# Gathers issued inside the routing stage, a LoRA product moved into the expert loop, and two pooling loads issued before the stage border

## The chip, the cores and the metric

The kernel runs on one core of a Trainium2 chip. A core has five engines that run side by side: PE (TensorE, matrix products), DVE (VectorE), ACT (ScalarE), POOL (GpSimd) and SP (SyncE, which here only issues DMAs). They talk through semaphores: an instruction may wait until a semaphore has reached a number, and raise one when it is done; a DMA raises one when its data has landed. The metric is device microseconds for one execution, lower is better. Times of before: 870.08 us, the median of 3 runs (869.97 to 871.64).

## The reference

Two layers work on x of 8 x 512 tokens with 512 channels. Layer 0 makes a LoRA feature of each token (by language), routes it to 2 of 8 experts with a capacity of 512 tokens each, and adds the experts' weighted outputs to x. Layer 1 is an attention-like pooling, followed by a quantised feed-forward network. Cut to the part that the change touches:

```
def _L0_ffn_ref(x, expert_embeddings, first_linear, second_linear):
    weights = _router(x, expert_embeddings)              # top 2 of 8, softmax
    ones = (weights > 0).astype(weights.dtype)
    cap_ones = jnp.where(jnp.cumsum(ones, axis=0) <= expert_capacity, ones, 0.0)
    caw = weights * cap_ones
    vals, idx = jax.lax.top_k(caw.T, expert_capacity)
    index = idx.reshape(-1)
    tokens = x_flat[index].reshape(E, expert_capacity, hidden)
    inter = jax.nn.relu(jnp.einsum('ech,eih->eci', tokens, first_linear))
    out = jnp.einsum('eci,ehi->ech', inter, second_linear) * vals[:, :, None]
    return jnp.zeros((n_tokens, hidden)).at[index].add(out.reshape(-1, hidden)).reshape(x.shape)
x = x + _L0_ffn_ref(_L0_cond_ref(x, ...), ...)           # _L0_cond_ref: LoRA, rank 16, plus embedding
x = _L1_cond_ref(x, ...)                                 # tanh scores, masked softmax, pooled / count
x = _L1_ffn_ref(x, ...)                                  # rmsnorm, int8 x ternary, gelu, int8 x ternary
```

## The kernel before

The program has four stages, each in a block of its own. At the end of a block every engine runs a DRAIN and then waits for all the others, so the next stage starts when the last engine has arrived.

**Routing.** The token features (64 LoRA coordinates and the language, 104 numbers a token) are computed from x for eight batches. The slots are then given in two halves, q = 0 and 1. For each half DVE chooses the experts (`choose`, which needs an exponential from ACT, `exps`), PE counts (`count`), DVE gives slots (`give_slots`), DVE and ACT build one-hot tables (`hot_lanes` on ACT), and PE inverts the map from token to slot (`find`). From that DVE makes `row_of_slot`, the token of each slot of each expert. POOL writes the features of a half to DRAM (L270) when they are complete, and waits at the end for both writes (L276, semaphore `feat_out`).

PE also computes, for each expert e, the product g of the first layer's weights with the LoRA matrix, 100 x 1024: `expand(e, n)` in two halves n of 512 columns, four fp32 products each (line L148). ACT stores its high part (`high_g`) and DVE its low part (`low_g`), so that later products run in a faster format with both parts. In the routing stage this is done for the experts 0 and 1.

**Experts.** At its start POOL gathers the feature rows of the experts 0 and 1 from DRAM with 4 indirect DMAs for each (L645). PE computes the product of expert 2 before it transposes the first gathered rows (`turn(0)`, L824). Then comes a loop over 8 experts and 8 blocks k of 128 inner channels: `inner_block` (L831, L832) makes 128 x 512 of the first layer, ACT and DVE split it into a high part (L728) and a low part (L793), and `out_block` (L844 to L846) adds 12 products of the second layer. From e = 1 on the loop also holds the product of expert e + 2, spread over the blocks by the table `G_AT`: `expand(e + 2, k)`, with one or two fp32 products behind the 12. The results are added to `x1_dram` by POOL's indirect DMAs (L659, semaphore `y_out`), and POOL waits for the last of them before the border.

**Pooling.** SP loads the masks (L949) and then two batches of x1 into `x_sum` (L954). DVE runs a chain of small operations (L1127 to L1154) that ends with the semaphore `setup`; PE waits for `setup` and for the first `x_sum` before its first transpose (L1035).

**Feed-forward.** 32 tiles of 128 tokens, not touched.

What sets the order is the written order on each engine: all engines run their instructions in the order of the text, and a waiting instruction holds back everything behind it on its engine.

Of the kernel before, what the change touches and what calls it, by code (L numbers as in the profile page):

```python
# [102 lines left out]
def build(nc, x, x_t, lang, kind, lora_a, lora_a_t, lora_b_t, embed_t, router_t, w_in_t, w_out_t,  # L103
# [7 lines left out]
    with ExitStack() as whole:  # L111
# [19 lines left out]

        l0 = whole.enter_context(ExitStack())
        row_of_slot = sb(l0, "row_of_slot", [P, EXPERTS * SB], U32)
        lora_b_sb = sb(l0, "lora_b_sb", [P, KD, STACK_1])
# [7 lines left out]
        feat_out, x1_init = sem("feat_out"), sem("x1_init")  # L142
        w_in_v = w_in_t.rearrange("e (p k) i -> e p k i", k=KD)
        w_out_v = w_out_t.rearrange("e (a k p) h -> e a p k h", a=2, p=P)

        def g_product(pe, e, n, k, bank):

            return pe.matmul(ps[0:STACK_1, bank, :], lora_b_sb[:, k, :],  # L148
                             w_in_sb[:, e % AHEAD, k, n * 512:(n + 1) * 512], start=k == 0, stop=k == KD - 1)


        with ExitStack() as a:
# [7 lines left out]
            xt = sb(a, "xt", [P, X_RING, KD, SEQ])  # L160
# [63 lines left out]
            with nc.Block() as block:  # L224
                @block.sync
                def _(sp):
# [5 lines left out]
                    def load_x(b):  # L232
                        if b >= X_RING:
                            sp.wait_ge(feats_mm, b - X_RING + 1)
                        sp.dma_start(xt[:, b % X_RING, :, :], xt_v[b]).then_inc(xt_in[b % X_RING], DMA)
# [24 lines left out]
                def _(pool):  # L260
# [15 lines left out]
                    pool.wait_ge(feat_out, DMA * PARTS)  # L276

                @block.scalar
                def _(act):
# [54 lines left out]
                    hot_lanes(0)  # L334
                    high_g(0, 0)
                    exps(1)
# [6 lines left out]
                def _(pe):  # L343
# [17 lines left out]
                    def feats(b):  # L361
# [4 lines left out]
                        for k in range(KD):  # L366
                            m = pe.matmul(ps[0:W, FEAT_T_BANK[b % 2], :], proj[:, b, k, :], xt[:, b % X_RING, k, :],
# [50 lines left out]
                    expand(0, 0)  # L418
                    expand(0, 1)
                    count(1)  # L420
                    expand(1, 0)
                    expand(1, 1)
                    find(1)

                @block.vector
                def _(ve):
# [123 lines left out]
                    ve.scalar_tensor_tensor(row_of_slot[:], spare[:], -1.0, token[:], ALU.add, ALU.add)  # L550
# [13 lines left out]
        with ExitStack() as a:  # L564
# [3 lines left out]
            rows = sb(a, "rows", [P, 2, SB, ROW])  # L568
# [15 lines left out]
            rows_in = [sem(f"rows_in{i}") for i in (0, 1)]  # L584
# [21 lines left out]
            with nc.Block() as block:  # L606
                @block.sync
                def _(sp):
# [9 lines left out]
                    for e in range(EXPERTS):  # L618
# [12 lines left out]
                        if e + AHEAD + 1 < EXPERTS:  # L631
                            n = e + AHEAD + 1
                            sp.wait_ge(g_mm, 2 * (n - AHEAD + 1))
                            sp.dma_start(w_in_sb[:, n % AHEAD, :, :], w_in_v[n]).then_inc(w_in_in[n % AHEAD], DMA)

                @block.gpsimd
                def _(pool):
                    pool.wait_ge(feat_out, DMA * PARTS)

                    def gather(e):  # L640
                        if e >= 2:
                            pool.wait_ge(rows_tr, e - 1)
                            pool.wait_ge(w_slot_ready, e - 1)
# [8 lines left out]
                    for e in range(EXPERTS):  # L652
                        if e + 2 < EXPERTS:
                            gather(e + 2)
# [803 lines left out]
```

## Time and profile before

| | |
|---|---|
| median of 3 runs | 870.08 us (869.97 to 871.64) |
| the profiled execution | 869.48 us |
| its span, first to last instruction | 867.3 us |
| granted TensorE clock, mean | 0.945 |
| PE busy | 760.5 us (88%) |
| DVE busy | 525.2 us (61%) |
| ACT busy | 503.6 us (58%) |
| POOL busy | 298.6 us (34%) |

The span is 2.2 us shorter than the execution that it was taken from; what lies around the span is not in the trace. All positions below are microseconds from the start of the span. The routing stage takes the first 86 us, the experts the time to 368.8 us, pooling the time to 601 us and the feed-forward network the rest. POOL's "DMA_INDIRECT" is the time in which POOL prepares a gather or scatter; the landing comes later. Names that end in q (POOLq) are the engine's sequencer. In the trace a product of line L148 appears as two MATMUL records.

### The profile page before, as it was taken

Reading aid. Unit: us, or ns where it says so; the run is one execution under the profiler, and the core shown is the slowest. Engines: PE = TensorE matmul, PEld = TensorE weight load, DVE = VectorE, ACT = ScalarE, POOL = GpSimd, SP = SyncE. Lnnn points to the kernel's source line nnn. Section 1 sums busy time; section 2 is a strip of 40 time slices with the busy share of each in tenths; the row PEclk is TensorE's granted clock in tenths of the full one; section 3 lists DMA queues with packets and bytes.
Section 4 is the critical chain, followed back from the end, with each engine's and each line's share of the span. In section 5 each row is a group of like instructions: output and inputs, shape, how many; then the busy total and the mean of one; then the engine's idle time right before and its main releaser. Section 6 shows DMA issues by size and latency. Waiting matters only on the chain. (4 is left out here: it accounts for less than half of the span.)

```text
span 867.3 us, 10854 instructions
## 1 busy us (share of the span) xinstructions
PE 760.5 (88%) x3794; PEld 492.9 (57%) x3824; DVE 525.2 (61%) x986; ACT 503.6 (58%) x714; POOL 298.6 (34%) x264
## 2 busy tenths in 40 slices
PE   6864899998999999246999999975799999999997
PEld 3331487776777777234777877763355555554553
DVE  2446344554544554132566565633899999999995
ACT  1144346753577788124655665522787777777783
POOL 0010324324224212213344444400354445544553
PEclk9987799999999999667999999987999999999999
DMA  7999359887558555331111120001012122122222
GB/s 231 373 400 336 123 202 335 268 288 205 170 134 211 153 146 132 48 128 50 49 49 48 50 98 1 1 1 36 6 57 73 61 74 74 62 65 70 74 64 82
DMA packets 42645, 109.03 MB, mean 126 GB/s; under 512 B 4320, under 2 KB 5104, under 8 KB 39392
## 3 DMA queue, kind: packets, MB, share of 16 engines
q1 hardware_dynamic: 35760, 94.84, 31.0%
q0 software_dynamic: 6320, 13.06, 8.1%
q8 instruction: 30, 0.49, 0.2%
q10 hardware_dynamic: 512, 0.45, 0.2%
q14 instruction: 23, 0.19, 0.1%
HBM read 88.59 MB, written 28.13 MB: 135 GB/s over the span
## 5 line engine op out<-in xcount | busy, mean ns | idle before, releaser
L1317 PE MATMUL ps<-ff_q,qt 128*128 128x512 bf16 x496 | 121.9, 386 | 8.4 <-DVE h L1382 6.3
L1343 PE MATMUL ps<-ff_q,ht 128*128 128x512 bf16 x498 | 114.5, 379 | 3.3 <-DVE ht L1399 2.6
L844 PE MATMUL ps<-w_h,inner_l 128*128 128x512 f32 x256 | 102.8, 402 | 3.6 <-DVE inner_l L793 3.6
L846 PE MATMUL ps<-w_h,inner_h 128*128 128x512 f32 x256 | 101.2, 395 | 0.0
L845 PE MATMUL ps<-w_l,inner_h 128*128 128x512 f32 x256 | 101.1, 395 | 0.0
L1303 POOL TENSOR_SCALAR hb<-h 128x2048 bf16<-128x2048 int8 x32 | 60.8, 1900 | 111.0 <-ACT h L1361 111.0
L659 POOL DMA_INDIRECT x_after_experts<-y,row_of_slot x32 | 51.5, 1609 | 134.6 <-DVE y L779 127.3
L1361 ACT ACTIVATE h<-h,to_q 128x2048 int8<-128x2048 f32 x32 | 64.1, 2002 | 44.1 <-DVE to_q L1413 44.1
L1382 DVE SCALAR_TENSOR_TENSOR h<-ps,scale,bias 128x1024 f32<-128x1024 f32 x64 | 81.6, 1279 | 9.1 <-PE ps L1317 9.0
L793 DVE SCALAR_TENSOR_TENSOR inner_l<-ps,inner_h 128x512 fp32r<-128x512 f32 x64 | 44.2, 691 | 70.1 <-ACT inner_h L728 69.6
L1317 PEld LDWEIGHTS ps<-ff_q,qt 128*128 128x128 bf16 x512 | 49.5, 99 | 63.9 <-DVE h L1382 7.6
L1343 PEld LDWEIGHTS ps<-ff_q,ht 128*128 128x128 bf16 x512 | 49.8, 98 | 62.7 <-DVE res L1422 1.6
L728 ACT ACTIVATE inner_h<-ps 128x512 fp32r<-128x512 f32 x64 | 38.0, 594 | 81.5 <-PE ps L832 81.1
L1387 DVE TENSOR_REDUCE mx<-h 128x1 f32<-128x1024 f32 x64 | 77.4, 1210 | 1.1 <-ACT h L1351 1.1
L1351 ACT ACTIVATE h<-h 128x1024 f32<-128x1024 f32 x64 | 67.1, 1049 | 16.1 <-DVE h L1382 16.1
L148 PE MATMUL ps<-w_in_sb,lora_b_sb 128*100 128x512 f32 x128 | 63.3, 617 | 9.7 <-PEq L224 9.7
L790 DVE TENSOR_TENSOR w_l<-w_raw,w_h 128x512 fp32r<-128x512 f32 x64 | 44.2, 690 | 45.2 <-ACT w_h L724 45.0
L1002 PE MATMUL ps<-x_h,prob_l 128*128 128x512 f32 x128 | 62.4, 488 | 6.5 <-ACT q L1097 6.4
L976 POOL TENSOR_TENSOR x_l<-x_sum,x_h 128x1024 fp32r<-128x1024 f32 x16 | 38.1, 2384 | 69.2 <-ACT x_h L1107 51.7
L1369 ACT ACTIVATE junk<-h 128x2048 bf16<-128x2048 f32 x32 | 61.1, 1911 | 1.0
L844 PEld LDWEIGHTS ps<-w_h,inner_l 128*128 128x128 f32 x256 | 49.1, 192 | 15.2 <-DVE inner_l L793 4.9
L846 PEld LDWEIGHTS ps<-w_h,inner_h 128*128 128x128 f32 x256 | 48.9, 191 | 10.8
(216 smaller groups left out, 1467.7 us busy)
## 6 DMA issues: line engine op xcount, KB each, us to landing
w_in_sb<-in_w_in_t SPq DMA_DIRECT2D x8, 2048.0 KB, 12.1
w_raw<-in_w_out_t SPq DMA_DIRECT2D x16, 1024.0 KB, 5.5
raw<-in_ff_t SPq DMA_DIRECT2D x16, 1024.0 KB, 7.5
xt<-in_x_t SPq DMA_DIRECT2D x8, 1024.0 KB, 9.4
x_after_experts<-in_x SPq DMA_DIRECT2D x8, 1024.0 KB, 18.0
x_sum<-x_after_experts SPq DMA_DIRECT2D x8, 1024.0 KB, 4.7
x<-x_after_experts SPq DMA_DIRECT2D x32, 256.0 KB, 2.7
out<-res SPq DMA_DIRECT2D x32, 256.0 KB, 2.0
```

Of the source, the lines that this page charges most:

```text
L148: return pe.matmul(ps[0:STACK_1, bank, :], lora_b_sb[:, k, :], w_in_sb[:, e % AHEAD, k, n * 512:(n + 1) * 512], start=k == 0, stop=k == KD ...
L844: pe.matmul(ps[:, s, :], inner_l[:, k % 2, c], w_h[:, k % RING, :], start=k == 0, stop=False)
L845: pe.matmul(ps[:, s, :], inner_h[:, k % 2, c], w_l[:, k % RING, :], start=False, stop=False)
L846: m = pe.matmul(ps[:, s, :], inner_h[:, k % 2, c], w_h[:, k % RING, :], start=False, stop=k == KI - 1)
L1002: pe.matmul(ps[:, NUM + j, :], prob_l[at_l], x_h[:, b % 2, l, :], start=first, stop=False)
L1317: m = pe.matmul(ps[:, f, :], qt[:, t, k, :], ff1_q[:, k, f * 512:(f + 1) * 512], start=k == 0, stop=k == KD - 1)
L1343: m = pe.matmul(ps[:, OUT[t3 % 2], :], ht[:, k, :], ff2_q[:, k, :], start=k == 0, stop=k == KF - 1)
L1351: act.activation(part, part, ACT.Gelu).then_inc(gelu, 1)
L1361: act.activation(h8[:, t1 % 2, :], h[:, t1 % 2, :], ACT.Copy, scale=to_q[:, t1 % 2:t1 % 2 + 1]).then_inc(h8_ready, 1)
L1369: act.activation(junk[:], h[:, t0 % 2, :], ACT.Square, accum_out=sq[:, t0 % 2:t0 % 2 + 1]).then_inc(h_sq, 1)
L1382: ve.scalar_tensor_tensor(h[:, t % 2, half], ff_bank[i], scale1[:, t:t + 1], bias1[:, half], ALU.mult, ALU.add).then_inc(biased, 1)
L1387: ve.tensor_reduce(mx[:, t % 2, i:i + 1], h[:, t % 2, i * HALF:(i + 1) * HALF], AX.X, ALU.max, apply_absolute_value=True).then_inc(h_max, 1)
```

## The change

The instructions that move, and what moves in memory with them:

- POOL issues the 8 gathers of the experts 0 and 1 at the end of the routing block, after `feat_out` and after a new semaphore `rows_known`, which DVE raises with `row_of_slot`. They no longer stand at the start of the expert block.
- ACT runs the second exponential `exps(1)` ahead of `high_g(0, 0)`; PE runs `count(1)` ahead of `expand(0, 1)`.
- PE runs `find(1)` ahead of `expand(1, 1)`.
- The product of expert 2 goes from the front of the expert block into the loop at e = 0, with its high and low parts.
- SP issues the first two `x_sum` loads at the end of the expert block, after a wait for all of `y_out`; the masks are loaded behind them, at the start of the pooling block.
- In memory, `rows` and `x_sum` live longer; two of the three buffers of x in the routing stage are now the `x_sum` buffers.

```diff
+        def gather(pool, e):
+            for s in range(SB):
+                pool.indirect_dma_start(
+                    rows[:, e % 2, s, :], None, feat_dram,
+                    bass.IndirectOffsetOnAxis(row_of_slot[:, e * SB + s:e * SB + s + 1], 0)).then_inc(rows_in[e % 2], DMA)
...
-            xt = sb(a, "xt", [P, X_RING, KD, SEQ])
+            xt = x_sum + [sb(a, "xt", [P, KD, SEQ])]
...
                     pool.wait_ge(feat_out, DMA * PARTS)
+                    pool.wait_ge(rows_known, 1)
+                    gather(pool, 0)
+                    gather(pool, 1)
...
                     hot_lanes(0)
+                    exps(1)
                     high_g(0, 0)
-                    exps(1)
                     high_g(0, 1)
...
                     expand(0, 0)
+                    count(1)
                     expand(0, 1)
-                    count(1)
                     expand(1, 0)
+                    find(1)
                     expand(1, 1)
-                    find(1)
...
-                    ve.scalar_tensor_tensor(row_of_slot[:], spare[:], -1.0, token[:], ALU.add, ALU.add)
+                    ve.scalar_tensor_tensor(row_of_slot[:], spare[:], -1.0, token[:], ALU.add, ALU.add).then_inc(rows_known, 1)
...
+                    sp.wait_ge(y_out, DMA * SB * EXPERTS)
+                    for b in (0, 1):
+                        load_x_sum(sp, b)
...
-                    pool.wait_ge(feat_out, DMA * PARTS)
-                    gather(0)
-                    gather(1)
                     pool.wait_ge(x1_init, DMA * BATCH)
...
-                    for n in (0, 1):
-                        high_g(AHEAD - 1, n, n)
                     take_rows(0)
...
-                            if k == 0 and 2 <= e <= EXPERTS - AHEAD + 1:
+                            if k == 0 and 1 <= e <= EXPERTS - AHEAD + 1:
                                 high_g(e + 1, 1)
-                            if k == 4 and 1 <= e <= EXPERTS - AHEAD:
+                            if k == 4 and e <= EXPERTS - AHEAD:
                                 high_g(e + 2, 0)
...
-                    low_g(AHEAD - 1, 0, 0)
                     take_rows(0)
-                    low_g(AHEAD - 1, 1, 1)
...
-                    pe.wait_ge(w_in_in[AHEAD - 1], DMA)
-                    for n in (0, 1):
-                        for k in range(KD):
-                            m = g_product(pe, AHEAD - 1, n, k, n)
-                        m.then_inc(g_mm, 1)
                     turn(0)
...
-                            if 1 <= e <= EXPERTS - AHEAD:
+                            if e <= EXPERTS - AHEAD:
                                 expand(e + 2, k)
...
                     sp.dma_start(mask[:], masks).then_inc(mask_in, DMA)
-                    for b in range(BATCH):
-                        if b >= 2:
-                            sp.wait_ge(x_trd, KD * (b - 1))
-                            sp.wait_ge(x_l_cp, 2 * (b - 1))
-                        sp.dma_start(x_sum[b % 2][:], x1_v[:, b * TPB:(b + 1) * TPB, :]).then_inc(x_in[b % 2], DMA)
+                    for b in range(2, BATCH):
+                        sp.wait_ge(x_trd, KD * (b - 1))
+                        sp.wait_ge(x_l_cp, 2 * (b - 1))
+                        load_x_sum(sp, b)
```

The order on PE from the last transposes of the routing stage to the first block of expert 0, before (L378 transposes features, L396 is `find`, L148 the LoRA product, L384 and L386 `count`, L224 and L817 the border, L824 `turn(0)`):

```order
L378 MATMUL ps<-const,feat_t 128x72 x8
L396 MATMUL ps<-ff_q 128x64 x32
L148 MATMUL ps<-w_in_sb,lora_b_sb 100x512 x8
L384 MATMUL ps<-chosen,ones_b 128x136
L386 MATMUL ps<-chosen,up_to_b 128x128
L148 MATMUL ps<-w_in_sb,lora_b_sb 100x512 x8
L396 MATMUL ps<-ff_q 128x64 x32
L224 UNCONDITIONAL_BRANCH
L817 UNCONDITIONAL_BRANCH
L148 MATMUL ps<-w_in_sb,lora_b_sb 100x512 x8
L824 MATMUL ps<-const,rows 100x128 x4
L831 MATMUL ps<-rows,g 128x512
```

The same place after the change, where L148 has become L158, L384 L405, L396 L417, L824 L831 and L831 L838:

```order
L399 MATMUL ps<-const,feat_t 128x72 x8
L417 MATMUL ps<-ff_q 128x64 x32
L158 MATMUL ps<-w_in_sb,lora_b_sb 100x512 x4
L405 MATMUL ps<-chosen,ones_b 128x136
L407 MATMUL ps<-chosen,up_to_b 128x128
L158 MATMUL ps<-w_in_sb,lora_b_sb 100x512 x8
L417 MATMUL ps<-ff_q 128x64 x32
L158 MATMUL ps<-w_in_sb,lora_b_sb 100x512 x4
L242 UNCONDITIONAL_BRANCH
L824 UNCONDITIONAL_BRANCH
L831 MATMUL ps<-const,rows 100x128 x4
L838 MATMUL ps<-rows,g 128x512
```

The second count now stands behind 4 products instead of 8, the second find ahead of the last 4, and the 8 products behind the border are gone. Two of them stand in the loop, on PE in expert 0 between the last products of `out_block(0, 0)` and `inner_block(0, 2)`:

```order
L849 MATMUL ps<-w_h,inner_l 128x512
L850 MATMUL ps<-w_l,inner_h 128x512
L851 MATMUL ps<-w_h,inner_h 128x512
L158 MATMUL ps<-w_in_sb,lora_b_sb 100x512 x2
L838 MATMUL ps<-rows,g 128x512
L839 MATMUL ps<-rows,g 128x512
```

The other six follow in the blocks k = 2 to 7 of expert 0, the way it was and is from expert 1 on. POOL before, from its last plain DMA of the routing stage, with what each waits for:

```order
L270 DMA token_features<-feat 128x1664 [waits placed,feat_cp]
L224 UNCONDITIONAL_BRANCH [waits feat_out,zero_out]
L636 UNCONDITIONAL_BRANCH [waits barrier_Pool_Activation_PE_DVE_SP_gather]
L645 DMA rows<-token_features,row_of_slot 128x104 [waits feat_out]
L645 DMA rows<-token_features,row_of_slot 128x104 x7
```

POOL after the change (L288 is the feature write, L164 a gather, L242 and L658 the border):

```order
L288 DMA token_features<-feat 128x1664 [waits placed,feat_cp]
L164 DMA rows<-token_features,row_of_slot 128x104 [waits rows_known,feat_out,zero_out]
L164 DMA rows<-token_features,row_of_slot 128x104 x7
L242 UNCONDITIONAL_BRANCH
L658 UNCONDITIONAL_BRANCH [waits barrier_Pool_Activation_PE_DVE_SP_gather]
L164 DMA rows<-token_features,row_of_slot 128x104 [waits w_slot_ready,rows_tr,x1_init]
```

All eight gathers now stand ahead of the border.

## Rows read from the trace of the kernel before

**Rows 1.** Windows of the trace; the columns are named in the row that is shown first.

```profile
core 0: us, PE busy (x) PEld busy (x) DVE busy (x) ACT busy (x) POOL busy (x), PEclk, DMA share, GB/s
77.00:86.10 9.10, 0.00 (x0) 0.00 (x0) 5.77 (x10) 0.39 (x1) 0.00 (x0) 0.50 1.01 360
86.10:89.30 3.20, 3.15 (x4) 1.27 (x5) 0.09 (x2) 0.00 (x0) 2.03 (x2) 0.50 0.90 283
100.60:106.30 5.70, 5.69 (x13) 4.46 (x14) 1.76 (x3) 0.04 (x1) 0.00 (x0) 0.50 0.00 0
123.00:156.00 33.00, 33.00 (x136) 24.52 (x135) 15.92 (x27) 20.33 (x38) 10.46 (x8) 1.00 0.86 293
```

**Rows 2.** Timeline of PE: start us, us, engine, line, what, [idle before, releaser].

```profile
56.28 8.21 PE L148 MATMUL ps<-w_in_sb,lora_b_sb 128*100 128x512 f32 x16
64.39 0.23 PE L384 MATMUL ps<-chosen,ones_b 128*128 128x136 bf16 x1
...
86.15 8.63 PE L148 MATMUL ps<-w_in_sb,lora_b_sb 128*100 128x512 f32 x16 [9.65 <-PEq L224]
94.66 0.65 PE L824 MATMUL ps<-const,rows 128*100 128x128 f32 x4
```

**Rows 3.** Timeline of ACT, end of the routing stage.

```profile
53.47 1.91 ACT L315 ACTIVATE ff_q<-ff_q 128x2048 bf16<-128x2048 bf16 x1
61.10 0.59 ACT L324 ACTIVATE g<-ps 64x512 fp32r<-64x512 f32 x1 [5.72 <-PE ps L148]
...
62.07 0.21 ACT L319 ACTIVATE gap_exp<-gap 128x16 f32<-128x16 f32 x1
...
68.74 4.78 ACT L312 ACTIVATE ff_q<-lane_id_b,minus_lo 128x128 bf16<-128x128 bf16 x16 [3.14 <-DVE minus_lo L521]
```

**Rows 4.** Timeline of DVE, end of the routing stage.

```profile
62.38 0.18 DVE L491 TENSOR_SCALAR kept<-gap_exp 128x16 f32<-128x16 f32 x1 [9.88 <-ACT gap_exp L319]
...
74.08 0.19 DVE L537 COPY feat<-slot 128x32 f32<-128x32 f32 x1
...
77.09 0.19 DVE L550 SCALAR_TENSOR_TENSOR row_of_slot<-spare,token 128x32 uint32<-128x32 f32 x1
```

**Rows 5.** Timeline of POOL, both sides of the border between the stages.

```profile
74.82 0.54 POOL L270 DMA_DIRECT2D token_features<-feat  x1 [22.99 <-DVE feat L537]
86.85 1.05 POOL L645 DMA_INDIRECT rows<-token_features,row_of_slot  x1 [11.49 <-POOLq L224]
...
95.75 0.95 POOL L645 DMA_INDIRECT rows<-token_features,row_of_slot  x1 [0.30 <-issue]
```

**Rows 6.** Line L270, both feature writes: issue to landing.

```profile
DMA to landing us min/median/max: 7.9/9.0/10.2
```

**Rows 7.** Line L224, the border after routing: names, count, ns, start us.

```profile
L224 POOLq DRAIN  x1: 645/645/645, 85.2 to 85.2; - x1
```

**Rows 8.** Line L606, the border after the experts.

```profile
L606 POOLq COMPARE_BRANCH  x1: 41/41/41, 363.1 to 363.1; - x1
L606 POOLq DRAIN  x1: 5273/5273/5273, 363.3 to 363.3; - x1
```

**Rows 9.** Timeline of PE, expert 0: the first second-layer product.

```profile
100.61 0.79 PE L844 MATMUL ps<-w_h,inner_l 128*128 128x512 f32 x1 [1.66 <-DVE inner_l L793]
```

**Rows 10.** Timeline of PE, expert 1: one part of a LoRA product in the loop.

```profile
137.05 1.02 PE L148 MATMUL ps<-w_in_sb,lora_b_sb 128*100 128x512 f32 x2
...
138.13 0.39 PE L832 MATMUL ps<-rows,g 100*128 100x512 f32 x1
138.37 0.60 PE L824 MATMUL ps<-const,rows 128*100 128x128 f32 x4
```

**Rows 11.** Timeline, start of the pooling stage.

```profile
369.15 49.92 SPq L954 DMA_DIRECT2D x_sum<-x_after_experts  x4
...
371.80 0.18 DVE L1154 CAST at_i<-at_f 128x32 int32<-128x32 f32 x1
...
375.04 1.94 PE L1035 MATMUL ps<-const,x_sum 128*128 128x128 f32 x8 [22.10 <-DMA x_sum<-x_after_experts]
```

More of the change, by code:

```diff
@@ L130, in build, with load_x_sum @@
         att_in = sem("att_in")
+        x_sum = [sb(whole, f"x_sum{i}", [P, TPB, D]) for i in (0, 1)]
+        x_in = [sem(f"x_in{p}") for p in (0, 1)]
+        x1_v = x1_dram[0:N_TOK, :].rearrange("(p t) d -> p t d", t=TILES)
+        def load_x_sum(sp, b):
+            sp.dma_start(x_sum[b % 2][:], x1_v[:, b * TPB:(b + 1) * TPB, :]).then_inc(x_in[b % 2], DMA)
         l0 = whole.enter_context(ExitStack())
         row_of_slot = sb(l0, "row_of_slot", [P, EXPERTS * SB], U32)
+        rows = sb(l0, "rows", [P, 2, SB, ROW])
         lora_b_sb = sb(l0, "lora_b_sb", [P, KD, STACK_1])
@@ L142, in build @@
         feat_out, x1_init = sem("feat_out"), sem("x1_init")
+        rows_known = sem("rows_known")
+        rows_in = [sem(f"rows_in{i}") for i in (0, 1)]
         w_in_v = w_in_t.rearrange("e (p k) i -> e p k i", k=KD)
@@ L634, in _ @@
                             sp.dma_start(w_in_sb[:, n % AHEAD, :, :], w_in_v[n]).then_inc(w_in_in[n % AHEAD], DMA)
+                    sp.wait_ge(y_out, DMA * SB * EXPERTS)
+                    for b in (0, 1):
+                        load_x_sum(sp, b)
                 @block.gpsimd
                 def _(pool):
-                    pool.wait_ge(feat_out, DMA * PARTS)
[L640 to L643, printed above, removed]
-                        for s in range(SB):
-                            pool.indirect_dma_start(
-                                rows[:, e % 2, s, :], None, feat_dram,
-                                bass.IndirectOffsetOnAxis(row_of_slot[:, e * SB + s:e * SB + s + 1], 0)).then_inc(rows_in[e % 2], DMA)
-                    gather(0)
-                    gather(1)
                     pool.wait_ge(x1_init, DMA * BATCH)
@@ L653, in _ @@
                         if e + 2 < EXPERTS:
-                            gather(e + 2)
+                            pool.wait_ge(rows_tr, e + 1)
+                            pool.wait_ge(w_slot_ready, e + 1)
+                            gather(pool, e + 2)
                         for s in range(SB):
@@ L796, in _ @@
                                 take_y(e - 1)
-                            if k == 0 and 2 <= e <= EXPERTS - AHEAD + 1:
+                            if k == 0 and 1 <= e <= EXPERTS - AHEAD + 1:
                                 low_g(e + 1, 1)
@@ L800, in _ @@
                                 weights(e)
-                            if k == 4 and 1 <= e <= EXPERTS - AHEAD:
+                            if k == 4 and e <= EXPERTS - AHEAD:
                                 low_g(e + 2, 0)
@@ L896, in build @@
         with ExitStack() as a:
-            x_sum = [sb(a, f"x_sum{i}", [P, TPB, D]) for i in (0, 1)]
             x_tr = sb(a, "x_tr", [P, 2, SEQ])
@@ L923, in build @@
             qb = sb(a, "qb", [P, TPB, KD, P], BF16)
-            x_in = [sem(f"x_in{p}") for p in (0, 1)]
             mask_in = sem("mask_in")
```

23 lines of the change are left out of this document (9 added, 14 removed).

## The prediction

> **What bounds the kernel now.** I read the windows first, then the timelines of the engines around the two stage borders that the change touches, then the borders' own rows. In the expert loop PE is the bound: from 123 to 156 us it is busy all 33.00 us at full clock [rows 1]. An operation added to PE in that loop costs its whole length, one taken away elsewhere gains only if PE waited for it. At the two borders PE is idle. From 77 to 86.1 us it does nothing while the DMA engines are fully busy (share 1.01) [rows 1]; it starts the product of expert 2 at 86.15 and the first transpose of gathered rows at 94.66 [rows 2]. At the other border it waits 22.10 us until 375.04, at last for the load of x_sum [rows 11]. So the change is three sums: when `turn(0)` can start, what the loop gets longer, and when the pooling stage can start.
>
> **The routing stage gets shorter by 3.4 us, as far as DVE.** DVE stood 9.88 us for the second exponential [rows 4], which ACT ran at 62.07, behind the high part that PE released at 61.10 [rows 3]. ACT is free at 53.47 + 1.91 = 55.4 and can now run it there. DVE then has `chosen` about 2 us later, near 57.7. That is no longer what ends last: `count(1)` now waits for PE, which is in `expand(0, 0)`. Its end releases ACT at 61.10, so the count now starts at about 61.0, against 64.39 [rows 2, 3]: 3.4 us sooner. DVE's chain from there is unchanged, so the last copy into the features moves from 74.08 to 70.7 and POOL's feature write from 74.82 to 71.4 [rows 4, 5]. ACT's second `hot_lanes` waits for the high part of (0, 1) (4 products of 0.86 us behind the count, then two copies of 0.59: 65.8) instead of for DVE until 68.74 [rows 3], so 2.9 us sooner; `find(1)` no longer has 4 products ahead of it that could hold it; so `row_of_slot` comes at 77.28 - 2.9 = 74.4 [rows 4]. The moved `expand(1, 1)` runs after it, from 73.7 at the latest to 80.6 (4 products of 1.7 us, if the clock has fallen), and its low part is done by 83.5; both lie beside POOL's work, below.
>
> **The border after routing: 2.3 us sooner for PE.** In before POOL passes its wait for the features at 85.0 and drains from 85.2 for 0.645 us [rows 7]; PE starts 86.15, 0.3 after the drain. So the landing of the second feature write holds this border: 74.82 + 10.2 = 85.0 [rows 5, 6]. The two writes took 7.9 and 10.2 us in the same full DMA traffic, median 9.0; issued at 71.4, the second lands at 79.3 to 81.6, and I take 80.4. `rows_known` (74.4) is then long there. POOL now issues 8 gathers before it can reach the border: 86.85 to 95.75 + 0.95 = 96.70, so 9.85 us [rows 5], plus 0.3 ahead of the first: 80.4 + 0.3 + 9.85 = 90.55. What stood behind the border, with only the first four gathers needed for `turn(0)`, now stands ahead of it with all eight. Then comes 0.15 and the drain. Its price with gathers before it is in no row. Two rows bound it: 0.645 us after the routing stage's 7 POOL DMAs (2 of features, 5 of zeros) [rows 7], and 5.27 us after the experts' 64 (32 gathers, 32 scatters), though the last had landed when it began [rows 8]. Per DMA that is 0.092 and 0.082 us, near enough to one law, so for 15 I take 1.3. With 0.3 to PE the border opens at 92.3, against `turn(0)` at 94.66 before: -2.3 us. The ends: landing 79.3 and a drain of 0.65 give 90.55, -4.1; landing 81.6 and a drain of 5.3 give 97.5, +2.8.
>
> The Trainium skill bears on the landing ("DMA: Bandwidth & Descriptors", section on queues, rings and completion order): each DMA engine takes turns between the rings that have work, a packet at a time. By that rule POOL's write isn't queued behind SP's backlog, and 3.4 us earlier in means about as much earlier out; if it were first in, first out over both queues, it would land with the backlog at 85. The 7.9 us of the first write, in the middle of that backlog, agree with the rule [rows 6].
>
> **From turn(0) to the first second-layer product: 0.5 us shorter.** Before, 94.66 to 100.61, 5.95 us [rows 2, 9]. Gone from it are ACT's high parts and DVE's low parts of expert 2, which stood between the steps; each such step is some 0.6 us on ACT [rows 3]. Against that the transposes and the first two products now run at the lower clock, since PE has idled since 77 and was at 0.50 there [rows 1]. Bounds 0 and 1.0 us; I take 0.5. The low clock of the first block (0.50 from 100.6 to 106.3 [rows 1]) stays about as long; each microsecond more or less of it is half a microsecond, so +-0.9.
>
> **The loop gets longer by 6.9 us.** Expert 0's blocks take over 8 fp32 products. In expert 1 one stands from 137.05 with two first-layer products behind it, the second at 138.13 and the next work at 138.37 [rows 10]: 1.32 less two of 0.24 = 0.84, and 0.86 if the two take the 0.23 that most take. 8 x 0.86 = 6.9 us. Before, they ran from 86.15 to 94.66 beside the gathers, where PE would have waited anyway: taking them from there gains nothing beyond the 2.3 above. In the loop nothing hides them: PE is the bound, and each stands behind the 12 products of an `out_block`, so none fits into the one wait of expert 0, 1.66 us [rows 9]. ACT and DVE have their parts of expert 2 in expert 0 and 1, as they have for later experts, in stretches where PE is busy without a gap [rows 1]. Bounds 6.7 and 7.7 (one product at the lower clock).
>
> **The border after the experts: 3.6 us sooner.** The wait for `y_out` ends at 363.1, but POOL's drain holds the border until 363.3 + 5.27 = 368.5 [rows 8]. SP issued x_sum at 369.15, after the masks, and PE started at 375.04 [rows 11], 5.9 later. SP now waits for `y_out` itself, issues at 363.2 and has x_sum at 369.0, under the drain. What is late next is `setup`: DVE ends it at 371.80 + 0.18 = 371.98 [rows 11], 3.2 us after the border. PE then starts at 372.05, -3.0. Eight DMAs fewer in this block take 8 x 0.08 = 0.65 off the drain, by the same law: -3.6. If the drain is fixed, -3.0. SP's two issues, 0.4 us each, end before 364.2, so SP is not late. The masks move behind x_sum; POOL needs them only behind ACT's first pass over x_sum, which itself waits for PE's first products.
>
> **Sum.** -2.3 - 0.5 + 6.9 - 3.6 = +0.5 us, against the profiled 869.48 us: 870.0. The median of the three runs is 0.6 above that execution, 870.08, so the forecast is 870.6 us.
>
> **Rivals.**
>
> *The drain is dear once there were gathers (slower).* For it: the only long drain stands behind indirect DMAs, none stands behind few of them. Against it: the count explains both rows. It decides from about 2.6 us of drain on (+1.3 us in the sum). At 5.3 us the routing border moves by +4.0 and the second keeps its 5.27 (+0.6): 875.2.
>
> *The feature write lands with the backlog, at 85.0 (slower).* `turn(0)` is then at 85.0 + 11.9 = 96.9, +4.6: 875.2. Against it is the first write's 7.9 us.
>
> *The routing is not shortened (slower).* If the count still ran at 64.4 (a lower clock of PE in `expand(0, 0)`, say), the feature write would stay at 74.8 and all of POOL's chain be 3.4 later: 874.0. Against it: rows 2 and 3 show ACT idle where the exponential goes.
>
> *The border is quicker than I have it (faster).* Landing at 79.3 (-1.1), a drain that doesn't grow (-0.65), the higher clock back sooner (-0.9): 868.0. For it: each part lies within its bound; against: they have to come together.
>
> **How the numbers follow.** The forecast's case has 0.60, the dear drain 0.17, the backlog 0.05, no shortening 0.06, the quick border 0.12. The first has a range of its own, 868.6 to 872.8. What this kernel's measurement can tell from no change is 0.2%, 1.7 us. Of the forecast's 0.60, 0.44 fall within that, 0.13 above it and 0.03 below. So faster 0.03 + 0.12 = 0.15, same 0.44, slower 0.13 + 0.28 = 0.41. The range runs from 868.0 to 875.2.
>
> **What will show it.** The count at 61.0, and DVE's wait of 9.88 us split in two of some 3 us, the second for PE; the feature write at 71.4, the first gather at 80.7 and the last at 89.6; POOL's drain at the first border 1.3 us, at the second 4.6; the first transpose of rows at 92.3; expert 0 longer by 6.9 us, the other experts as long as before; x_sum issued right behind the last scatter's landing, and PE's first transpose there released by DVE's setup, not by a DMA. I am wrong if the drain doesn't follow the count of DMAs, or if expert 0 grows by much less than 6.9.

## The result, and the profile after

| | kernel before | changed kernel |
|---|---|---|
| median, same chip, 7 runs each | 870.41 us (868.44 to 871.64) | 875.97 us (871.79 to 877.70) |
| ratio of after to before | | 1.006, 95% interval 1.004 to 1.008 |
| profiled execution: span | 867.3 us | 875.0 us |
| `turn(0)` starts | 94.66 | 98.24 |
| first second-layer product of expert 0 | 100.61 | 103.94 |
| last second-layer product of expert 7 | 352.55 | 364.11 |

The change costs 0.6%, about 5.5 us where 0.5 was forecast, and the time lies 0.8 us above the range. In the two profiled executions the difference is 7.7 us: 3.6 up to `turn(0)`, -0.25 from there to the first second-layer product, 8.2 in the loop, -3.9 from the start of its last product to the end. The medians differ by 5.6; the profiled execution of the changed kernel is one of its slower ones (877.18).

Timeline of DVE after (start us, us, engine, line, what, [idle before, releaser]), answering [rows 4]:

```profile
57.37 0.17 DVE L512 TENSOR_SCALAR kept<-gap_exp 128x16 f32<-128x16 f32 x1 [3.10 <-ACT gap_exp L340]
...
63.47 0.44 DVE L525 TENSOR_TENSOR_SCAN running<-not_first,ps 128x136 f32<-128x136 f32 x1 [4.14 <-PE ps L407]
...
72.82 0.19 DVE L558 COPY feat<-slot 128x32 f32<-128x32 f32 x1
...
76.10 0.19 DVE L571 SCALAR_TENSOR_TENSOR row_of_slot<-spare,token 128x32 uint32<-128x32 f32 x1
```

The wait of 9.88 us has split in two as forecast, the second one for PE. The count was expected at 61.0 and its result is used at 63.47. This execution runs 1.4 us late before the chain starts (the first feature write goes out at 49.4 against 48.05); the other microsecond is the chain's own.

Timeline of POOL after, answering [rows 5]:

```profile
73.56 0.54 POOL L288 DMA_DIRECT2D token_features<-feat  x1 [20.37 <-DVE feat L558]
85.98 1.05 POOL L164 DMA_INDIRECT rows<-token_features,row_of_slot  x1 [11.89 <-DMA token_features<-feat]
...
94.85 0.94 POOL L164 DMA_INDIRECT rows<-token_features,row_of_slot  x1 [0.30 <-issue]
```

Line L288, both feature writes from issue to landing ([rows 6] before), and line L242, the border after routing ([rows 7] before; name, count, ns, start):

```profile
DMA to landing us min/median/max: 8.2/9.9/11.6
```

```profile
L242 SPq DRAIN  x1: 122/122/122, 83.2 to 83.2; - x1
L242 POOLq DRAIN  x1: 9011/9011/9011, 89.0 to 89.0; - x1
```

The write goes out 1.3 us sooner than before and lands at 73.56 + 11.6 = 85.1, where it landed before (85.0). The first gather is at 85.98 and the last ends at 95.79. POOL's drain ends at 97.96, 2.2 us later. The row starts at 89.0 although POOL still issues gathers then, so its length is no measure of the wait; its end is.

Timeline of PE after, the first transpose of rows, the first second-layer product and one LoRA product in expert 0 ([rows 2, 9, 10] before):

```profile
98.24 1.07 PE L831 MATMUL ps<-const,rows 128*100 128x128 f32 x4 [17.77 <-PEq L242]
...
103.94 0.79 PE L849 MATMUL ps<-w_h,inner_l 128*128 128x512 f32 x1 [0.56 <-DVE inner_l L800]
...
114.08 1.02 PE L158 MATMUL ps<-w_in_sb,lora_b_sb 128*100 128x512 f32 x2
114.53 0.79 PE L838 MATMUL ps<-rows,g 128*128 128x512 f32 x1
```

Windows of the two traces from the first to the last of those products, first of before, then of after. The columns are us, busy us and instructions of each engine, granted clock of PE, DMA share, GB/s:

```profile
100.61:352.60 251.99, 247.11 (x1002) 186.44 (x1002) 123.17 (x204) 157.64 (x269) 69.98 (x53) 0.98 0.65 193
```

```profile
103.94:364.16 260.22, 255.35 (x1018) 189.70 (x1018) 126.05 (x208) 160.21 (x274) 70.16 (x53) 0.98 0.63 189
```

The loop has 16 PE instructions more, the 8 fp32 products. PE idles as long as before (4.88 and 4.87 us) and is busy 8.2 us longer. Not all of that is the products. Windows of before and of after, behind the same stall of 2.9 us in expert 3:

```profile
198.50:201.90 3.40, 3.35 (x9) 2.77 (x10) 1.88 (x3) 0.00 (x0) 3.05 (x2) 0.50 0.93 264
```

```profile
208.10:214.90 6.80, 6.13 (x15) 4.80 (x16) 2.47 (x5) 0.51 (x1) 3.89 (x3) 0.50 1.03 264
```

The granted clock falls to 0.50 (1.2 GHz) for 3.4 us in one execution and for 6.8 in the other.

The border after the experts ([rows 8, 11] before): line L625 first, then the timeline of the start of pooling.

```profile
L625 POOLq COMPARE_BRANCH  x1: 44/44/44, 374.5 to 374.5; - x1
L625 POOLq DRAIN  x1: 4622/4622/4622, 374.7 to 374.7; - x1
```

```profile
374.52 0.82 SPq L137 DMA_DIRECT2D x_sum<-x_after_experts  x2
379.55 0.33 SPq L946 DMA_DIRECT2D mask<-in_masks  x1
382.59 0.18 DVE L1150 CAST at_i<-at_f 128x32 int32<-128x32 f32 x1
...
382.82 1.54 PE L1031 MATMUL ps<-const,x_sum 128*128 128x128 f32 x6 [18.32 <-DVE at_i L1150]
```

This step came out as forecast: x_sum is issued under the drain, the drain is 0.65 us shorter with 8 DMAs fewer, PE is released by DVE's setup. From the wait's end to PE it is 8.3 us, against 11.9.

### The profile page after: what moved, and what is told of

Read it like the earlier page. It is cut to its first block and busy times, and to the rows that moved or that the text cites. A ratio compares the mean times of both kernels' runs of the same rounds, so it can differ in the third digit from the quotient of the medians.

```text
span 875.0 us, 10854 instructions
## 1 busy us (share of the span) xinstructions
PE 765.8 (88%) x3794; PEld 494.1 (56%) x3824; DVE 525.1 (60%) x986; ACT 503.4 (58%) x714; POOL 298.3 (34%) x264
## 5 line engine op out<-in xcount | busy, mean ns | idle before, releaser
L1378 DVE SCALAR_TENSOR_TENSOR h<-ps,scale,bias 128x1024 f32<-128x1024 f32 x64 | 81.6, 1279 | 9.0 <-PE ps L1313 8.9
L158 PE MATMUL ps<-w_in_sb,lora_b_sb 128*100 128x512 f32 x128 | 65.0, 623 | 0.0
L164 POOL DMA_INDIRECT rows<-token_features,row_of_slot x32 | 31.4, 980 | 73.7 <-DVE w_slot L773 54.2
## 6 DMA issues: line engine op xcount, KB each, us to landing
w_in_sb<-in_w_in_t SPq DMA_DIRECT2D x8, 2048.0 KB, 12.4
```

The lines of the kernel that those rows point to most:

```text
L1378: ve.scalar_tensor_tensor(h[:, t % 2, half], ff_bank[i], scale1[:, t:t + 1], bias1[:, half], ALU.mult, ALU.add).then_inc(biased, 1)
```

## The experiments

Each kernel ran in five rounds beside the kernel before, on one of three chips, where the kernel before had medians of 870.73 us (`only_loads`, `only_order`, `only_loop`, `copies_held`), 871.25 (`product_routing`, `gather_split`, `before_held`, `all_four`) and 871.67 (`two_edits`, `gathers_behind`). A ratio is to the kernel before, with its 95% interval. Microseconds "less than" or "above" another version are differences of medians; where the two ran on different chips the ratios are the safer comparison. "Profile" is one execution of each; times in it are us of its span.

**The three parts alone, on the kernel before.** First the pooling loads (`only_loads`):

```diff
+                    sp.wait_ge(y_out, DMA * SB * EXPERTS)
+                    for b in (0, 1):
+                        load_x_sum(sp, b)
```

The pooling block keeps its loads from the third batch on, and `x_sum` lives as long as in the changed kernel.

> The kernel before with one part of the change: SP waits for all of y_out and issues the first two x_sum loads before the border after the experts. Theory (POOL's drain still 5.27 us for 64 DMAs, then DVE's setup is what ends last): PE's first transpose 3.0 us sooner relative to the last scatter's landing, released by DVE; 3.0 us less in all, 867.4 against 870.4. Rival (the early loads are worth nothing, since PE waits for the setup at much the same time, or the drain gets longer with SP's loads beside it): within 0.5 us of before.

Measured: 868.0 us, ratio 0.9971 (0.9948 to 0.9994), so -2.5 us. In the profile POOL's wait ends at 362.5, its drain is 5273 ns as before, and PE starts 8.9 us behind the wait, 3.0 less than before:

```profile
371.39 1.97 PE L1041 MATMUL ps<-const,x_sum 128*128 128x128 f32 x8 [19.39 <-DVE at_i L1160]
```

The early loads are worth 3 us, and the other 0.65 of the 3.6 comes from the eight gathers that have left the block.

Then the routing stage's order (`only_order`):

```diff
                     hot_lanes(0)
-                    high_g(0, 0)
                     exps(1)
+                    high_g(0, 0)
...
                     expand(0, 0)
-                    expand(0, 1)
                     count(1)
+                    expand(0, 1)
                     expand(1, 0)
-                    expand(1, 1)
                     find(1)
+                    expand(1, 1)
```

> The kernel before with one part of the change: the second exponential before the first high part on ACT, the second count one half product earlier and the second find ahead of the last four products on PE. Theory A (POOL's second feature write lands when SP's eight copies of x are nearly through, whenever it is issued): issued near 71.5, landed at 84 to 85.5, the border after routing where it was, within 1 us of before. Theory B (landing follows the issue by 8 to 10 us, as I predicted): landed at 80 to 81.6, the border near 83.5 (then held by DVE's low parts), about 2.5 to 3 us less in all.

Measured: 871.12 us, ratio 1.0007 (0.9985 to 1.0029): nothing. In the profile the write goes out at 72.08, 2.7 us sooner than before, and takes 12.4 us. Line L270, both writes, then PE:

```profile
DMA to landing us min/median/max: 8.4/10.4/12.4
```

```profile
85.62 9.31 PE L148 MATMUL ps<-w_in_sb,lora_b_sb 128*100 128x512 f32 x16 [6.72 <-PEq L224]
96.04 0.65 PE L824 MATMUL ps<-const,rows 128*100 128x128 f32 x4 [1.11 <-DMA rows<-token_features,row_of_slot]
```

It lands at 84.5, 0.5 us sooner than before. Most of what DVE wins is lost in the flight. The rest is lost behind the border: PE starts 0.5 us sooner, but the fourth gather lands 9.7 us behind the start of the first (7.8 before), and `turn(0)` is at 96.04 against 94.66.

Then the product (`only_loop`), which leaves the place behind the border and goes into expert 0, with its high and low parts (not shown):

```diff
-                    for n in (0, 1):
-                        for k in range(KD):
-                            m = g_product(pe, AHEAD - 1, n, k, n)
-                        m.then_inc(g_mm, 1)
...
-                            if 1 <= e <= EXPERTS - AHEAD:
+                            if e <= EXPERTS - AHEAD:
                                 expand(e + 2, k)
```

> The kernel before with one part of the change: the product of expert 2 and its parts inside the loop at e = 0, the gathers still behind the border. Theory (eight fp32 products of 0.86 us on a full PE; turn(0) still released by the landing of the first four gathers at 94.6): 6.9 us more, less 0.5 us for the shorter chain behind turn(0), and up to 0.9 more if PE's clock comes back later: 876.0 to 878, that is +6 to +7.5. Rival (the larger clock loss of the changed kernel is what costs, and the products themselves mostly fit beside waits of PE): +1 to +3.

Measured: 881.3 us, ratio 1.0113 (1.0088 to 1.0137), so +9.8 us (7.7 to 11.9): more than I expected. In its profile `turn(0)` is at 94.71, as before, since the gathers hold it now:

```profile
94.71 1.09 PE L820 MATMUL ps<-const,rows 128*100 128x128 f32 x4 [18.75 <-DMA rows<-token_features,row_of_slot]
```

So the product behind the border was free, and in the loop it is not.

**What the product costs.** Twelve profiles give the loop's length and, within it, how long the granted clock stood at 0.50:

| kernel | loop us | at 0.50, us |
|---|---|---|
| all_four, before_held, product_routing | 249.2, 249.3, 249.2 | 3.1, 3.2, 3.2 |
| only_loads | 249.5 | 3.8 |
| before, only_order | 251.9, 251.9 | 9.1, 9.1 |
| gathers_behind, two_edits | 252.7, 252.9 | 11.3, 11.6 |
| product inside: copies_held | 256.8 | 4.0 |
| product inside: gather_split | 259.3 | 9.6 |
| product inside: changed kernel, only_loop | 260.2, 260.3 | 12.0, 12.2 |

Without the product the loop grows from 249.2 to 252.8 over 8.2 us of low clock, 0.44 us for each. At equal low clock (4.0, 9.6, 12.0) the kernels with the product inside are longer by 7.2, 7.1 and 7.1 us. The forecast had 6.9. The changed kernel's other 1.3 of 8.2 us is 2.9 us more of low clock, and the product is not what brings it: behind the stall `copies_held` has none and `gather_split` 3.4 with the product inside, `gathers_behind` and `two_edits` have the 6.8 without it. It differs from profile to profile. That still doesn't explain all 9.8 us of `only_loop`, whose interval begins 0.6 above the 7.1. Its profiled span is 11.1 us longer than that of the kernel before: 8.4 lie in the loop (7.1 and 1.3 as above), 0.4 from the loop's last product to PE's first transpose of pooling, and 2.5 behind that, where the two programs have the same text. From that transpose to the end the twelve profiles spread from 491.7 to 494.8 us, the kernel before at 492.3, `only_loop` at 494.8. So about 2.5 us of the surplus lie outside the code that was edited; why that stretch varies stays open.

**The copies held** (`copies_held`). On the changed kernel, SP lets the last four of its eight copies of x wait until the feature write has landed:

```diff
+                        if b == 4:
+                            sp.wait_ge(feat_out, DMA * PARTS)
                         sp.dma_start(x1_rows
```

> The changed kernel, but SP issues only four of its eight copies of x to x1 before it waits for feat_out; the other four come behind the feature write. Theory A (the feature write is slowed by the copies beside it): the second write lands 5 to 8 us after its issue, at 79 to 81, the gathers start there and turn(0) comes 4 to 6 us sooner than in the changed kernel; 870 to 872 in all. Theory B (what delays the landing is POOL's own queue, or the write itself): landing still 10 to 12 us after the issue, 876 as the changed kernel.

Measured: 872.12 us, ratio 1.0015 (0.9999 to 1.0031), 3.9 us less than the changed kernel. Timeline of POOL, then line L290 (both feature writes), lines L242 and L164 (the gathers, from the start of their issue to landing):

```profile
70.84 0.54 POOL L290 DMA_DIRECT2D token_features<-feat  x1 [19.39 <-DVE feat L560]
76.56 1.05 POOL L164 DMA_INDIRECT rows<-token_features,row_of_slot  x1 [5.19 <-DMA token_features<-feat]
...
85.45 0.95 POOL L164 DMA_INDIRECT rows<-token_features,row_of_slot  x1 [0.30 <-issue]
```

```profile
DMA to landing us min/median/max: 4.9/6.4/8.0
```

```profile
L242 POOLq DRAIN  x1: 12847/12847/12847, 79.5 to 79.5; - x1
```

```profile
DMA to landing us min/median/max: 6.2/6.5/7.1
```

The write now takes 4.9 us instead of 11.6: the copies beside it are what slows it. That it goes out sooner in this execution is not the reason: in `gather_split` it goes out at 70.92, beside the copies, and takes 11.7. This is theory A, and `turn(0)`, at 92.66, is 5.6 us sooner. But the border opens only at 92.4, 6 us behind the last gather's end (86.4). The gathers in turn fly beside the held copies, 6.2 to 7.1 us, the last landing at 91.7; the drain ends 0.7 us behind that. A drain that counts DMAs would have ended at about 87.7, by the forecast's 1.3. So with gathers before it POOL's drain lasts until they have landed. The last held copy lands at 91.7 too, but it isn't what the drain waits for: in the kernel before the drain is over at 85.9 and the eighth copy lands at 87.95.

**The gathers split** (`gather_split`). On the changed kernel the second four gathers go behind the border:

```diff
                     gather(pool, 0)
-                    gather(pool, 1)
...
+                    gather(pool, 1)
                     pool.wait_ge(x1_init, DMA * BATCH)
```

> The changed kernel with the four gathers of the second batch moved behind the border; the first four stay in the routing stage. Theory A (the barrier waits until the gathers issued before it have landed): the fourth gather ends at about 90.8, lands at about 92.5, the drain ends about 0.8 us later, and turn(0) is at about 93.5 instead of 98.2; the second four, issued from 94 on, are landed long before their turn at 138. Time about 871.3, 4.5 us under the changed kernel. Rival B (the drain costs by the number of DMAs issued in the block, 0.08 us each): it saves 0.3 us beside the 5 us of issuing, turn(0) at 93.0. Rival C (POOL is not what holds the barrier): turn(0) stays within 1 us of 98.2 and the time within 1 us of 876.

Measured: 870.03 us, ratio 0.9985 (0.9969 to 1.0002), 6 us less than the changed kernel.

```profile
L242 POOLq DRAIN  x1: 5659/5659/5659, 84.6 to 84.6; - x1
```

```profile
90.54 1.07 PE L831 MATMUL ps<-const,rows 128*100 128x128 f32 x4 [12.90 <-PEq L242]
```

The fourth gather ends at 88.3, the last landing in the trace before the border is at 89.75, the drain ends at 90.3. First gather to `turn(0)` is 7.1 us instead of 12.3: four gathers' issue of 1.25 us each, and 0.2. The rest of the 7.7 us by which `turn(0)` is sooner is the write, which lands at 82.6 in this execution. Rival C is out. A and B lie only 0.5 us apart here, so this run doesn't tell them apart; `copies_held` does.

**The product in the routing stage** (`product_routing`). On the changed kernel:

```diff
                     find(1)
                     expand(1, 1)
+                    expand(2, 0)
+                    expand(2, 1)
...
-                            if e <= EXPERTS - AHEAD:
+                            if 1 <= e <= EXPERTS - AHEAD:
                                 expand(e + 2, k)
```

> The changed kernel with the LoRA product of expert 2 taken out of the loop and put at the end of the routing stage, behind the halves of expert 1, where the profile after the change has TensorE idle from 80.5 to 98.2 us. Everything else stays. Theory A (the product inside the loop is what the loop pays for, and the routing stage can hide it): the product takes 8.5 us at the granted clock of that stretch, so TensorE is done at about 89.5 and VectorE at about 92, both before the gathers' drain ends at 98.05; turn(0) stays at 98.2; the loop is shorter by 7 to 8 us (first out product to last product start 260.2 to about 252.5), time about 868.5 (1.5 to 2.5 us under the kernel before, 7 to 8 under the changed one). Rival B (the barrier waits for the product's halves): turn(0) moves to 100 or later and the gain is 5 us or less, 871 or more. Rival C (the loop's surplus is TensorE's clock and not the product): the loop shortens by under 5 us.

Measured: 867.95 us, ratio 0.9964 (0.9950 to 0.9978), 8.0 us less than the changed kernel.

```profile
75.86 12.19 PE L158 MATMUL ps<-w_in_sb,lora_b_sb 128*100 128x512 f32 x24
97.68 1.06 PE L835 MATMUL ps<-const,rows 128*100 128x128 f32 x4 [9.64 <-PEq L242]
```

All the products run in what was PE's idle time and end at 88.1, 9.6 us before PE is wanted. The loop is 11.0 us shorter in the profile; at 0.44 us for each us of low clock, 3.9 of that is 8.9 us less at 0.50, and 7.1 the product.

**The copies held, on the kernel before** (`before_held`), with the same two new lines:

> The kernel before with one edit: the last four of SyncE's eight copies of x wait until the feature write has landed. Theory A (the write is slowed by those copies, and the border waits for the write): it lands at about 80 instead of 85.0 (issued 74.8, 4.9 us in the held variant of the changed kernel), the border then waits for VectorE until about 82.7, and turn(0), with the product of 8.5 us in front of it, comes at about 91.5 instead of 94.7: time 867 to 868, 3 us under the kernel before. Rival B (the copies held end later than the border and delay what follows, the gathers above all): turn(0) within 1 us of 94.7, time 870 to 871.

Measured: 877.76 us, ratio 1.0075 (1.0051 to 1.0099): 6.5 us slower where I expected 3 faster. Both theories missed; B's place was right, its price far too low. The border (line L224), the timeline of SP, and that of PE:

```profile
L224 POOLq DRAIN  x1: 645/645/645, 80.7 to 80.7; - x1
...
L224 SPq DRAIN  x1: 123/123/123, 87.7 to 87.7; - x1
```

```profile
59.20 23.96 SPq L255 DMA_DIRECT2D x_after_experts<-in_x  x5
83.20 2.04 SPq L256 DMA_DIRECT2D kind_i<-in_kind  x1
```

```profile
88.12 8.80 PE L148 MATMUL ps<-w_in_sb,lora_b_sb 128*100 128x512 f32 x16 [9.90 <-PEq L224]
102.89 1.09 PE L826 MATMUL ps<-const,rows 128*100 128x128 f32 x4 [5.97 <-DMA rows<-token_features,row_of_slot]
```

The write lands at 80.5, in 3.7 us, and POOL is at the border at 80.7. But SP, which issues its four copies and four small loads only then, comes at 87.7 and now holds it. The first gather starts at 88.8, 2.0 us later than before, and from there to `turn(0)` it takes 14.1 us instead of 7.8, as the gathers fly beside the held copies. The transfer is not gone, it has moved onto the gathers. In the changed kernel SP stays clear of the path, since the border waits for the gathers anyway.

**Three edits together** (`all_four`, the changed kernel with `product_routing`, `gather_split` and `copies_held`):

> The changed kernel with three edits together: expert 2's LoRA product at the end of the routing stage, the second four gathers behind the border, and the last four of SyncE's eight copies of x held until the feature write has landed. Theory A: the write lands at about 76, the four gathers are issued from 76.6 to 81.5 and landed by 87, TensorE's products end at about 87 and VectorE's part at about 90, so that turn(0) is at 90 to 91 (98.2 in the changed kernel, 94.7 before); the loop is 7 to 8 us shorter than the changed kernel's; the second border keeps its 3.6 us. Time 861 to 863. Rival B (what is won at the border comes back in the loop as waits for weights, since the copies and the gathers now lie beside the weight loads): 866 or more, with new waits of TensorE for weights in the loop.

Measured: 859.33 us (858.74 to 859.82), ratio 0.9863 (0.9842 to 0.9885): 12 us faster than the kernel before, 1.4%, and the fastest version. Line L242 and PE:

```profile
L242 POOLq DRAIN  x1: 9765/9765/9765, 78.5 to 78.5; - x1
L242 SPq DRAIN  x1: 122/122/122, 84.2 to 84.2; - x1
...
L242 DVEq DRAIN  x1: 1425/1425/1425, 87.4 to 87.4; - x1
```

```profile
89.14 0.62 PE L837 MATMUL ps<-const,rows 128*100 128x128 f32 x4 [2.86 <-PEq L242]
```

POOL is done at 88.3 and DVE, with the low parts of expert 2, at 88.8: the two sides meet, and PE waits 2.9 us instead of 17.8. No wait for weights has come into the loop.

**Without holding the copies** (`two_edits`, the `all_four` version without the two `copies_held` lines):

> The changed kernel with two of the three edits of the fastest version so far (859.3 us): expert 2's LoRA product at the end of the routing stage, and the second four gathers behind the border. SyncE's copies of x are not held. Theory A (the held copies win only what the feature write lands sooner, the rest of that version's gain is from the two other edits): the write lands at about 84.5, the four gathers run from 85.3 to 90, they have landed at about 92 and the barrier ends at about 92.5 (6.9 us behind the first gather in the run with the split gathers alone), so turn(0) at about 92.7 against 89.1 with the copies held; the loop is 249.2 us. Time 862.5 to 864, 3 to 4 us over the fastest. Rival B (holding the copies gives the four gathers nothing, as VectorE's part holds the barrier): turn(0) at 89 to 90 and time 860 or less.

Measured: 862.24 us, ratio 0.9885 (0.9861 to 0.9909), 2.9 us above `all_four`. `turn(0)`:

```profile
92.36 0.98 PE L835 MATMUL ps<-const,rows 128*100 128x128 f32 x4 [4.71 <-PEq L242]
```

It is 3.2 us later, where theory A had 3.6. By the ratios the gap between the two versions is 1.9 us and not 2.9, and their intervals overlap; the profile shows the mechanism, the size is uncertain by a microsecond or two.

**All gathers behind the border** (`gathers_behind`, the `product_routing` version with both calls of `gather` moved):

```diff
-                    gather(pool, 0)
-                    gather(pool, 1)
...
+                    gather(pool, 0)
+                    gather(pool, 1)
                     pool.wait_ge(x1_init, DMA * BATCH)
```

> The changed kernel with expert 2's LoRA product at the end of the routing stage and all eight gathers issued behind the border, as in the kernel before; the earlier exponentials, the moved count and the early pooling loads stay. Theory A (gathers inside the routing stage are worth what their issue and flight lie beside the products): the barrier ends with VectorE's part at about 90.6, the first gather starts at about 91.5, and the fourth has landed about 8 us later (93.98 to 94.61 against a first gather at 86.85 in the kernel before), so turn(0) comes at about 99 to 99.5, later than the 97.7 of the version with all eight inside. Loop 249.2 us, time 869 to 870, 1 to 2 us over the version with all eight inside (867.95). Rival B (with the product in front of the border, the place of the gathers does not matter within 1 us): 868 or less.

Measured: 869.3 us, ratio 0.997 (0.9957 to 0.9984), 1.3 us above `product_routing`. Line L242 and PE:

```profile
L242 POOLq DRAIN  x1: 645/645/645, 84.9 to 84.9; - x1
...
L242 DVEq DRAIN  x1: 1425/1425/1425, 88.2 to 88.2; - x1
```

```profile
98.56 1.09 PE L835 MATMUL ps<-const,rows 128*100 128x128 f32 x4 [11.56 <-DMA rows<-token_features,row_of_slot]
```

With no gathers before it POOL's drain is 645 ns again. `turn(0)` is 0.9 us later than in `product_routing`. By the ratios the two are 0.5 us apart, with intervals of 1.2 us on either side. All eight gathers inside the routing stage, the change's first idea, are thus worth at most about 1 us with the product out of the way, and rival B, that the place does not matter within 1 us, stands.

## Why the prediction was wrong

**The step that failed: "issued at 71.4, the second lands at 79.3 to 81.6".** It went out at 73.56 and landed at 85.1. I had taken a flight of 7.9 to 10.2 us to hold for an earlier issue. Without held copies it lands at 82.6 to 85.1 in nine kernels, issued anywhere from 70.9 to 74.8, and takes 10.2 to 12.4 us. With the copies held it takes 3.7 to 4.9 us.

Part of that spread is a late or early start of the execution. Measured from the landing of the eighth copy in the same trace, the write goes out 13.1 to 13.6 us ahead of it in three kernels with the old order (before, `only_loads`, `only_loop`) and lands 2.9 to 3.0 ahead; in three with the new order (changed kernel, `only_order`, `gathers_behind`) it goes out 15.6 to 16.8 ahead and lands 4.0 to 5.0 ahead. So of 2.3 to 3.5 us sooner in, 1.1 to 2.1 came out again: about half.

This was the rival "lands with the backlog", to which I had given 0.05: it says `turn(0)` at 96.9 and 875.2 us; measured were 98.24 and 875.97. Its number came true, its mechanism only in part: the write does not queue behind the copies. In before the eighth copy was issued at 69.39 and landed at 87.95, the write was issued at 74.82 and landed at 84.97. The first write's 7.9 us rightly spoke against such a queue (the first copy, issued 14 us ahead of it, landed 9 us behind it), but it said nothing on whether a flight stays the same when it starts sooner.

The Trainium skill's rule that a DMA engine takes turns between its rings, a packet at a time ("DMA: Bandwidth & Descriptors", section on queues, rings and completion order), agrees with that overtaking. But I drew from it that sooner in means as much sooner out, and here that was false.

**The border after routing** was off by 5.9 us (92.3 against 98.24). The landing is 4.7 of it: the write went out 2.2 us later than forecast, of which 1.4 is the late start, and flew 2.6 us longer than the 9.0 taken. The first gather followed the landing by 0.84 us instead of 0.3, another 0.5. The drain ended 2.2 us behind the last gather instead of 1.45, 0.7 more; PE followed it by 0.3, as forecast. The law of 0.08 us for each DMA holds where everything has landed (4.62, 4.95 and 5.27 us for 56, 60 and 64 at the second border) and fails where gathers are in flight. In the changed kernel that is worth under 1 us; in `copies_held`, where the first gather starts 9.4 us sooner, it takes 3.8 of them back.

**The routing stage itself** came shorter as far as DVE, but not by a steady 3.4 us: the write goes out 2.7 us sooner in `only_order`, 4.0 and 3.9 in `copies_held` and `gather_split`, 1.3 in the changed kernel's profile, with its late start. Of what was won here about half was lost in the flight.

**From `turn(0)` to the first product:** 5.70 us against 5.95, -0.25 where I had -0.5.

**The loop:** the term was right, 7.1 us at equal clock against 6.9. The profile showed 8.2, and 1.3 of it was the low clock behind the stall in expert 3, which I had not allowed to vary. My ±0.9 covered the first block only.

**The border after the experts** was right to the tenth from the wait's end to PE: -3.6, by x_sum under the drain, a drain by count, and DVE's setup last.

Sum: forecast -2.3 - 0.5 + 6.9 - 3.6 = +0.5; profile +3.6 - 0.25 + 8.2 - 3.9 = +7.7. The late start (1.4) and the clock (1.3) belong to this execution and not surely to the change; the medians differ by 5.6.

What the prediction never asked is where else the product could go. I wrote that it ran before "beside the gathers, where PE would have waited anyway", and priced its move at 6.9 us, rightly; the savings at the two borders, 5.9 us by my own sum, could not pay for it. `product_routing` shows the place where it is free once the gathers are inside the routing stage: before the border.

## What to carry to other kernels

Work that stands beside a wait is free there and costs its whole length in a saturated loop; if the wait moves, move the work with it, not into the loop. A flight time read beside a saturating queue is no constant: ask when that queue runs dry before you credit an earlier issue, and when you hold the queue back, look at what it will meet next and who issues it (`before_held`). Put only those gathers ahead of a stage border that the next stage needs first, since the border waits for all of them to land.

## What was unexpected of the hardware

- POOL's drain at a border lasts until the gathers before it have landed: it ended 0.5 to 0.8 us behind the last landing in the six traces with gathers ahead of it (changed kernel 97.14 and 97.96, `copies_held` 91.71 and 92.38, `gather_split` 89.75 and 90.26, `all_four` 87.73 and 88.23). Without gathers in its block it was 645 ns. The profile has it on the border's line only, as a row of the engine's queue.
- A write of 832 KB on POOL's queue took 3.7 to 4.9 us with SP's copies held and 10.2 to 12.4 us beside them.
- The same stall of 2.9 us in expert 3 is followed by 0, 3.4 or 6.8 us at a granted clock of 0.50, in different profiles (five, three and four of the twelve). Each microsecond of it costs this loop 0.44 us: `product_routing` and `two_edits`, whose loops have the same text, differ by 3.6 us there, 3.0 of it by this.
